# Column sums on GpSimd, spills issued by SyncE, softmax division on VectorE, in a perceiver block

## The chip, the cores and the metric

One Trainium2 chip, one core. The time is the device time of one execution in microseconds (us). Another execution was taken with the hardware profiler. It has its own time and a trace. Engines: TensorE (PE), VectorE (DVE), ScalarE (ACT), GpSimd (POOL) and SyncE (SP, which only issues DMAs).

## The reference, cut to what matters

For 16 batches (NB) of 64 latent rows (LQ) and 512 context rows (S), width 512 (D), everything float32:

```
ln  = layernorm(layernorm(x)) * g_l + b_l          # 1024 latent rows in all
xn  = layernorm(ctx) * g_x + b_x
q   = ln @ w_q ;  k, v = split(concat(xn, ln) @ w_kv)
x  += layernorm(softmax(q k^T / 8) v @ w_out) * g_o + b_o      # 8 heads of 64
x  += differential_attention(layernorm(x))
x  += fp4_ffn(layernorm(x))                        # weights quantised in blocks of 16
```

Two parts bear on the change. The layernorm of the context is folded into the weights: a context key is `rstd * (ctx @ Wf)`, with `Wf = g_x * w_kv - mean over rows of (g_x * w_kv)`. The folding needs the column sums of `g_x * w_kv`. The shift `b_x @ w_v` is carried as one more value row. In the same way, part of the latent norm's shift is taken out of the queries and comes back as the vector `b_x @ w_q` ("queries' shift").

## The kernel before, in words

Every engine runs one program written out by hand. The order of a program is the order of its work. Engines wait on counting semaphores only, so an instruction that waits holds up all that stands behind it on its engine. SP is such a program too: a DMA issue that waits holds up every later DMA of SP. Products that need accuracy are done as three passes of rounded halves (`mm3`, L142: hi*hi, hi*lo, lo*hi), with ACT rounding to `hi` and DVE subtracting to get `lo`.

**Stage A** (latents) ends about 92 us into the span. SP loads x in four tiles and one block of four, and then w_kv. ACT issues the four loads of w_q. DVE takes statistics and norms x, PE turns it (`turn_first_latents`, L471), and `first_queries` (L481) makes the first half of the queries. Between its chunks stand sixteen narrow float32 matmuls (L487) for the queries' shift. Then come keys and values of the latents, second half of everything, and `weight_means` (L522), an `mm3` of 12 matmuls per half of w_kv that gives the column sums in two PSUM rows. ACT copies these to `mean_row`. SP writes them to DRAM and reads them back spread over all partitions (`spill_means`, `spread_means`), and `fold_weight` on DVE (L917) uses them. Queries, latent keys and values go to DRAM scratch. POOL issues 20 of these spills (`spill_query` for both halves, `spill_latent_key` and `spill_latent_value` for the first) as soon as each is ready. SP issues the last eight, after `load_pack(0)`.

The SP program of stage A, in order: loads; context rows 0 (waits for the second half's turned latents); context columns 0; masks and constants; context rows 1; `spill_rstd(0)`, a write of 512 single floats; `spread_rstd(0)`, which waits for that write to land; `load_pack(0)`, which waits for all spills of queries and for those of the first half's keys and values; the last spills; context columns 1; w_out.

**Stage B** (cross attention) has 16 batches of 8 slots. Slots 0 to 3 project keys, slots 4 to 7 project values and make scores. One slot is 12 matmuls of 512 columns and small work. The softmax of head pair n of a batch goes through three slots. In slot n+4 PE makes scores, DVE takes the row maximum (`largest`, L938) and ACT the exponent. In slot n+5 DVE inverts the sum (`invert_sum`, L948) and ACT multiplies 128x576 by it (`normalise_p`, L1515), and in slot n+6 PE turns the result. Beside it, 34 tiles of ffn weights are quantised on DVE, 4 steps per slot. Each is turned on PE, split by ACT (`hi_of_weight`, L1555) and DVE (`lo_of_weight`, L1042), and POOL spills both halves with two DMAs (`spill_weight`, L1863). `hi_of_weight` waits for the spills of the tile before, since they share buffers. A tile is split at slot 4, 7 or 0 of an odd batch and at slot 2 or 5 of an even one.

In slot 3 of batch 0, DVE waits for all spills of stage A to land and then clears buffers that lie on their place (`zero_pack(1)`, L1240, called at L1310). Behind it on DVE stand the last keys and the first `largest`, which frees the PSUM bank for PE's second scores.

In each batch SP issues, in slot 4, the next context rows and `spill_rstd` (L1988), and in slot 5 `spread_rstd` (L1993), which waits for that write. `scale_k` of the next batch needs the result.

Stages C to E (differential attention, ffn) have no part in the change.

## Time and profile before

| | |
|---|---|
| time, median of 3 runs | 995.66 us (992.62 to 996.56) |
| the profiled execution's own time | 999.49 us |
| its span, first to last instruction | 997.7 us |
| PE busy | 954.4 us, 96% |
| DVE busy | 772.9 us, 77% |
| ACT busy | 440.2 us, 44% |
| POOL busy | 144.9 us, 15% |
| granted TensorE clock, mean | 0.995 |

PE's ends are modelled and overlap, so the share of busy time says less than the list of its waits. The clock is at 2.4 GHz except for two stretches, one of them in the middle of stage B.

### The profile page before, as it was taken

The numbers are of one execution on the slowest core, as the hardware profiler recorded it, in microseconds if no ns is written. First come the engines' busy times: TensorE is split into PE (matmuls) and PEld (weight loads), VectorE is DVE, ScalarE is ACT, GpSimd is POOL, SyncE is SP. The second block draws the span as 40 slices with busy tenths as digits, with TensorE's granted clock in tenths as the row PEclk, the third lists the DMA queues.
The fourth block names the chain that finished last, engine by engine and source line by source line (L and its number), as shares of the span: only waits on it lengthen the run. The fifth ranks groups of instructions, "written<-read, shape, count | busy, mean of one in ns | idle before, by whom it ended". The sixth has DMA issues, their size and how long they took to land.

```text
span 997.7 us, 16573 instructions
## 1 busy us (share of the span) xinstructions
PE 954.4 (96%) x6364; PEld 776.7 (78%) x6364; DVE 772.9 (77%) x1653; ACT 440.2 (44%) x848; POOL 144.9 (15%) x166
## 2 busy tenths in 40 slices
PE   5999899999999979999999999999999999999997
PEld 4778788787888868787888887777777678888885
DVE  6555677798788858887887884578888588999984
ACT  4533654664465445466446644633324322222221
POOL 1220011211111111111211211022322000000000
PEclk9999999999999999999999999999999999999999
DMA  5788576756667563685676557160001730000000
GB/s 213 197 251 186 160 143 151 164 111 181 162 111 183 136 164 99 155 169 118 169 155 148 120 141 184 39 222 23 1 1 59 289 118 11 11 11 11 11 11 21
DMA packets 91994, 120.04 MB, mean 120 GB/s; under 512 B 47366, under 2 KB 56198, under 8 KB 89612
## 3 DMA queue, kind: packets, MB, share of 16 engines
q1 hardware_dynamic: 83980, 93.30, 32.7%
q0 software_dynamic: 7360, 24.65, 13.2%
q8 instruction: 50, 0.82, 0.4%
q10 hardware_dynamic: 576, 1.05, 0.3%
q14 instruction: 28, 0.23, 0.1%
HBM read 89.04 MB, written 29.93 MB: 119 GB/s over the span
## 4 chain that ended last, share of the span: by engine, by line
PE 65%; DVE 15%; DMA 7%; issue 6%; ACT 5%; POOL 1%; SPq 0%; DVEq 0%; ACTq 0%
PE ps_banks L146 16%; PE ps_banks L148 15%; PE ps_banks L147 15%; PE ps_banks L462 5%; DMA scratch_rstd<-sb_rstd_b 4%; PE ps_banks L580 3%; PE ps_banks L661 3%; PE ps_banks L728 2%; PE ps_banks L729 2%; PE ps_banks L730 2%; DVE sb_kfull L894 1%; DVE sb_kT_lo L865 1%; DMA scratch_wdn<-sb_w_lo 1%; DVE sb_b_stats L826 1%; PE ps_banks L495 1%
## 5 line engine op out<-in xcount | busy, mean ns | idle before, releaser
L1430 ACT ACTIVATE sb_kT_hi<-sb_kfull 128x512 fp32r<-128x512 f32 x64 | 40.5, 632 | 164.5 <-DVE sb_kfull L894 164.5
L146 PE MATMUL ps_banks<-sb_zT_hi,sb_wkv_hi 128*128 128x512 f32 x256 | 106.9, 418 | 0.3 <-DVE sb_kfull L894 0.3
L148 PE MATMUL ps_banks<-sb_zT_hi,sb_wkv_lo 128*128 128x512 f32 x256 | 100.9, 394 | 0.0
L147 PE MATMUL ps_banks<-sb_zT_lo,sb_wkv_hi 128*128 128x512 f32 x256 | 100.4, 392 | 0.0
L147 PE MATMUL ps_banks<-sb_wkv_lo,sb_zT_hi 128*128 128x512 f32 x256 | 100.3, 392 | 0.0
L146 PE MATMUL ps_banks<-sb_wkv_hi,sb_zT_hi 128*128 128x512 f32 x256 | 100.1, 391 | 0.0
L148 PE MATMUL ps_banks<-sb_wkv_hi,sb_zT_lo 128*128 128x512 f32 x256 | 100.0, 390 | 0.0
L945 DVE CUSTOM_DVE_ANT_0 sb_probs<-ps_banks,sb_maskbias 128x576 f32<-128x576 f32 x64 | 48.1, 751 | 34.1 <-PE ps_banks L148 33.7
L146 PE MATMUL ps_banks<-sb_wgu,sb_z_hi 128*128 128x512 f32 (+1 forms) x192 | 73.7, 384 | 0.0
L147 PE MATMUL ps_banks<-sb_wgu,sb_z_hi 128*128 128x512 f32 (+1 forms) x192 | 72.1, 375 | 0.0
L148 PE MATMUL ps_banks<-sb_wgu,sb_z_lo 128*128 128x512 f32 (+1 forms) x192 | 72.0, 375 | 0.0
L894 DVE TENSOR_TENSOR sb_kfull<-ps_banks,sb_rstd_row 128x512 f32<-128x512 f32 x64 | 43.6, 681 | 26.6 <-PE ps_banks L148 17.2
L1517 ACT ACTIVATE sb_probs<-sb_probs,sb_row_inv 128x576 f32<-128x576 f32 x64 | 49.6, 775 | 27.7 <-DVE sb_row_inv L953 27.1
L148 PEld LDWEIGHTS ps_banks<-sb_zT_hi,sb_wkv_lo 128*128 128x128 f32 x256 | 48.4, 189 | 11.1
L146 PEld LDWEIGHTS ps_banks<-sb_zT_hi,sb_wkv_hi 128*128 128x128 f32 x256 | 48.5, 189 | 10.8 <-DVE sb_kfull L894 0.6
L865 DVE TENSOR_TENSOR sb_zT_lo<-sb_ctxT,sb_zT_hi 128x512 fp32r<-128x512 f32 x64 | 43.7, 687 | 16.2 <-ACT sb_zT_hi L1430 15.1
L148 PEld LDWEIGHTS ps_banks<-sb_wkv_hi,sb_zT_lo 128*128 128x128 f32 x256 | 48.1, 188 | 10.5
L1505 ACT ACTIVATE sb_v<-ps_banks,sb_rstd_b 128x512 f32<-128x512 f32 x64 | 43.6, 681 | 27.5 <-PE ps_banks L148 27.3
L147 PEld LDWEIGHTS ps_banks<-sb_zT_lo,sb_wkv_hi 128*128 128x128 f32 x256 | 48.7, 190 | 8.6
L146 PEld LDWEIGHTS ps_banks<-sb_wkv_hi,sb_zT_hi 128*128 128x128 f32 x256 | 48.0, 188 | 8.5
L147 PEld LDWEIGHTS ps_banks<-sb_wkv_lo,sb_zT_hi 128*128 128x128 f32 x256 | 48.0, 188 | 8.1
L1512 ACT ACTIVATE sb_probs<-sb_probs,sb_neg_max 128x576 f32<-128x576 f32 x64 | 49.4, 772 | 1.7 <-DVE sb_neg_max L945 1.4
(263 smaller groups left out, 2435.3 us busy)
## 6 DMA issues: line engine op xcount, KB each, us to landing
sb_ctx<-in_ctx SPq DMA_DIRECT2D x16, 1024.0 KB
sb_ctxT<-in_ctx_t SPq DMA_DIRECT2D x16, 1024.0 KB, 8.4
sb_wgu<-scratch_wgu SPq DMA_DIRECT2D x8, 1024.0 KB, 9.7
scratch_wgu<-sb_w_hi POOLq DMA_DIRECT2D x22, 256.0 KB
scratch_wgu<-sb_w_lo POOLq DMA_DIRECT2D x22, 256.0 KB
sb_wdn<-scratch_wdn SPq DMA_DIRECT2D x2, 2816.0 KB, 9.7
scratch_q<-sb_a_qk POOLq DMA_DIRECT2D x8, 512.0 KB, 7.2
sb_rstd_row<-scratch_rstd SPq DMA_DIRECT2D x16, 256.0 KB, 4.8
```

Of the source, the lines that this page charges most:

```text
L146: e.matmul(o, wh, xh, start=i == 0, stop=False)
L147: e.matmul(o, wh, xl, start=False, stop=False)
L148: m = e.matmul(o, wl, xh, start=False, stop=i == n - 1)
L462: m = e.transpose(psum[:, bank, k * P:(k + 1) * P], s, ident[:, :])
L580: m = e.matmul(o_space(r, n), value, p_t[j][:, k, r], start=k == CS, stop=k == CS - 1)
L865: e.tensor_tensor(lo, full, hi.bitcast(F32), ALU.subtract).then_inc(done)
L894: e.tensor_tensor(k_full[n % 2][:, :], psum[:, bank, :], rstd_row[:, :], ALU.mult).then_inc(drained[bank])
L945: e.tensor_tensor_reduce(blocks(probs[j][:, :], WIDE // 2), s_space[j], blocks(mask_bias[:, keys(b)], WIDE // 2), -1.0, F32_MAX, ALU.add, ...
L1430: e.activation(dst, src, ACT.Identity).then_inc(done)
L1505: e.activation(v_sb[b % 2][:, k, :], psum[:, bank, :], ACT.Identity, scale=rstd_b[:, b % 2, k:k + 1]).then_inc(drained[bank])
L1512: e.activation(probs[j][:, :], probs[j][:, :], ACT.Exp, bias=neg_max[:, n:n + 1], scale=-1.0, accum_out=row_sum[b % 2][:, n:n + 1]).then_i ...
L1517: e.activation(probs[n % 2][:, :], probs[n % 2][:, :], ACT.Copy, scale=row_inv[:, n:n + 1]).then_inc(p_normed)
```

## The change

- Column sums: POOL multiplies each of the four 128x512 chunks of w_kv by its column of g_x (and of b_x for the values) and adds them up (`weighted_sum`): three sums of 7 instructions. One float32 matmul of 128x128 ones against 128x512 then gives each sum on all partitions. `copy_means` becomes one ACT copy of 128x512 with scale 1/D, straight to `mean_all`. The DMAs of the means go. `b_x @ w_v` is a third such matmul at the end of stage A, and ACT copies it to its row of the value buffers.
- The queries' shift: all sixteen matmuls stand behind the first transposes, and DVE's reduction stands before it norms the second half.
- Tiles 0 and 2 of x and chunks 0 and 2 of w_q go by SP, tiles 1 and 3 and chunks 1 and 3 by ACT.
- All spills of POOL are issued by SP. The first half's queries and latent keys stand behind the load of context columns 0, the latent values behind the constants, the second half's queries behind `spread_rstd(0)`. A weight tile is spilled one slot after its split, behind what SP has in that slot.
- `normalise_p` moves from ACT to DVE: reciprocal and multiplication, now behind `largest` of the same slot.

```diff
             def turn_first_latents():
                 banks = [claim(("lnT", 0, c), ring_a) for c in range(C)]
+                shift_bank = claim(("qs",), ring_a)
...
+                for k in range(C):
+                    on.wait_ge(wq_landed[k], 16)
+                    for n in range(C):
+                        m = e.matmul(psum[:, shift_bank, n * C + k:n * C + k + 1], w_raw[:, k, n * P:(n + 1) * P], cols[:, 1, k:k + 1], start=True, stop=True)
+                m.then_inc(filled[shift_bank])
...
             def weight_means(part):
-                mm3(e, psum[0:2, bank, :], lambda c: (gb_hi[:, :, c], gb_lo[:, :, c]),
-                    lambda c: (wkv_hi[:, c, cs], wkv_lo[:, c, cs]), range(C)).then_inc(filled[bank])
+                on.wait_ge(g_summed, part + 1)
+                e.matmul(psum[:, bank, :], ones[:, :], sum_g[:, part * D:(part + 1) * D], start=True, stop=True).then_inc(filled[bank])
...
-            def invert_sum(b, n):
+            def normalise_p(b, n):          # on DVE
                 on.wait_ge(exped, idx + 1)
                 e.reciprocal(row_inv[:, n:n + 1], row_sum[i][:, n:n + 1]).then_inc(row_inverted)
+                on.wait_ge(row_inverted, idx + 1)
+                e.tensor_scalar(probs[j][:, :], probs[j][:, :], row_inv[:, n:n + 1], None, ALU.mult).then_inc(p_normed)
...
-                    if old and slot == 0:
-                        invert_sum(b - 1, 3)
-                    if cur and slot >= 5:
-                        invert_sum(b, slot - 5)
                     if cur and slot >= 4:
                         largest(b, slot - 4)
+                    if old and slot == 0:
+                        normalise_p(b - 1, 3)
+                    if cur and slot >= 5:
+                        normalise_p(b, slot - 5)
...
+            def weighted_sum(out, weights, gain, done):     # on POOL
+                for c in range(C):
+                    if c == 0:
+                        e.tensor_scalar(out, weights[:, 0, :], gain[:, 0:1], None, ALU.mult).then_inc(pool_chain.up())
+                        continue
+                    on.wait_ge(pool_chain.sem, pool_chain.value)
+                    e.tensor_scalar(term[:, :], weights[:, c, :], gain[:, c:c + 1], None, ALU.mult).then_inc(pool_chain.up())
+                    on.wait_ge(pool_chain.sem, pool_chain.value)
+                    e.tensor_tensor(out, out, term[:, :], ALU.add).then_inc(done if c == C - 1 else pool_chain.up())
...
             # SP, stage A
-            spill_means(0)
             load_rows(0)
-            spread_means(0)
             load_columns(0)
+            for n in range(C):
+                spill_query(0, n)
+            for n in range(C):
+                spill_latent_key(0, n)
             load_mask(0)
...
-            spill_means(1)
-            spread_means(1)
+            for k in range(4):
+                spill_latent_value(0, k)
             load_rows(1)
             spill_rstd(0)
             spread_rstd(0)
+            for n in range(C):
+                spill_query(1, n)
...
             # SP, stage B, in each slot
+                    if turned is not None:
+                        spill_weight(turned)
+                    turned = None
                     for job, step in WEIGHTS.get((b, slot), ()):
+                        if step == SPLIT_STEP:
+                            turned = job
                         if step == TURN_STEP and job + 2 < NJ:
                             load_weight(job + 2)
```

## Rows read from the trace of the kernel before

**Rows 1.** Waits of PE: us in total, times, longest us.
```profile
PE ps_banks L462 <- DVE sb_w_lo L865: 7.1, 1, 7.1
PE ps_banks L146 <- DVE sb_tile_lo L958: 4.6, 6, 1.1
```

**Rows 2.** Chain that ended last, the first 30 us: start us, us, what.
```profile
2.11 6.42 DMA sb_a_x<-in_x
...
10.48 3.02 PE ps_banks L477 x13
...
15.83 2.96 PE ps_banks L495 x12
18.80 0.79 PE ps_banks L487 x8
```

**Rows 3.** Timeline of PE: start us, us, instruction.
```profile
40.54 0.40 PE L146 MATMUL ps_banks<-sb_wkv_hi,sb_a_gb_hi 128*2 128x512 f32 x1
...
686.94 3.24 PE L661 MATMUL ps_banks<-sb_dwo,sb_tT 128*128 128x512 f32 x7 [0.41 <-ACT sb_tT L1623]
```

**Rows 4.** Timeline of SP, end of stage A and batch 0.
```profile
66.95 0.43 SPq L1990 DMA_DIRECT2D scratch_rstd<-sb_rstd_b  x1
83.21 0.32 SPq L131 DMA_DIRECT2D sb_rstd_row<-scratch_rstd  x1
...
88.85 3.93 SPq L131 DMA_DIRECT2D scratch_klat<-sb_a_qk  x4
...
109.80 0.33 SPq L131 DMA_DIRECT2D sb_ctx<-in_ctx  x1
111.30 0.38 SPq L1990 DMA_DIRECT2D scratch_rstd<-sb_rstd_b  x1
...
121.23 0.33 SPq L131 DMA_DIRECT2D sb_rstd_row<-scratch_rstd  x1
```

**Rows 5.** DMA issues: count, KB each, median us to landing.
```profile
scratch_klat<-sb_a_qk SPq DMA_DIRECT2D x4, 512.0 KB, 5.4
```

**Rows 6.** A stretch of stage A: us; busy PE, PEld, DVE, ACT, POOL; clock; DMA share; GB/s.
```profile
40.40:106.00 65.60, 65.60 (x302) 52.08 (x300) 36.30 (x70) 24.89 (x42) 7.84 (x11) 1.00 0.86 239
```

**Rows 7.** Timelines of DVE and PE in batch 0, at the clearing.
```profile
102.32 0.48 DVE L1242 MEMSET sb_qpack<- 64x512 uint32 x1
...
106.98 0.40 PE L146 MATMUL ps_banks<-sb_kT_hi,sb_qpack 128*128 128x288 f32 x1 [0.62 <-DVE sb_neg_max L945]
```

**Rows 8.** Batches 6, 7 and 8 of stage B, columns as in rows 6.
```profile
293.15:329.00 35.85, 35.20 (x241) 28.69 (x240) 29.80 (x72) 19.62 (x40) 6.19 (x8) 1.00 0.68 160
329.00:361.45 32.45, 32.45 (x235) 27.01 (x234) 28.58 (x68) 18.78 (x38) 5.25 (x6) 1.00 0.54 137
361.45:405.77 44.32, 37.03 (x241) 30.33 (x240) 30.08 (x73) 19.80 (x40) 6.76 (x9) 0.92 0.52 128
```

**Rows 9.** Timelines of POOL and ACT at the long stall.
```profile
363.08 0.71 POOL L131 DMA_DIRECT2D scratch_wgu<-sb_w_lo  x1 [11.00 <-issue]
...
370.52 0.60 ACT L1430 ACTIVATE sb_w_hi<-ps_banks 128x512 fp32r<-128x512 f32 x1 [10.30 <-DMA scratch_wgu<-sb_w_lo]
```

**Rows 10.** Waits on SP and ACT, whole span: us in total, times, longest.
```profile
SPq L131 <- DMA scratch_rstd<-sb_rstd_b: 159.7, 15, 15.8
ACT sb_w_hi L1430 <- DMA scratch_wgu<-sb_w_lo: 21.1, 5, 10.3
```

**Rows 11.** Groups by line: busy us, mean ns, idle us before them.
```profile
L839 DVE TENSOR_SCALAR sb_y_row<-sb_y_row,sb_lo_mv,sb_lo_rstd 128x512 f32<-128x512 f32 x7 | 3.8, 538 | 0.0
...
L1517 ACT ACTIVATE sb_probs<-sb_probs,sb_row_inv 128x576 f32<-128x576 f32 x63 | 48.8, 775 | 26.4 <-DVE sb_row_inv L953 25.8
...
L1876 POOL TENSOR_TENSOR sb_by_cos<-sb_by_cos,sb_by_sin 128x512 f32<-128x512 f32 x16 | 20.6, 1286 | 44.9 <-DVE sb_by_cos L1085 44.9
```

**Rows 12.** Timeline of DVE and PE in slot 6 of batch 7.
```profile
352.70 0.76 DVE L945 CUSTOM_DVE_ANT_0 sb_probs<-ps_banks,sb_maskbias 128x576 f32<-128x576 f32 x1 [0.58 <-PE ps_banks L148]
...
355.25 0.60 PE L462 MATMUL ps_banks<-sb_ident,sb_probs 128*128 128x128 f32 x4
```

More of the change, by code:

```diff
@@ L522, in weight_means, with value_shift @@
             def weight_means(part):
-                cs = slice(part * D, (part + 1) * D)
-                on.wait_ge(gb_lo_split, 1)
-                on.wait_ge(w_lo_split, part + 1)
+                on.wait_ge(g_summed, part + 1)
                 bank = claim(("gw", part), ring_a)
-                mm3(e, psum[0:2, bank, :], lambda c: (gb_hi[:, :, c], gb_lo[:, :, c]),
-                    lambda c: (wkv_hi[:, c, cs], wkv_lo[:, c, cs]), range(C)).then_inc(filled[bank])
+                e.matmul(psum[:, bank, :], ones[:, :], sum_g[:, part * D:(part + 1) * D], start=True, stop=True).then_inc(filled[bank])
+            def value_shift():
+                on.wait_ge(bv_summed, 1)
+                bank = claim(("vs",), ring_a)
+                e.matmul(psum[:, bank, :], ones[:, :], sum_bv[:, :], start=True, stop=True).then_inc(filled[bank])
             def project_k(b, n):
@@ L1736, in scalar_program @@
                 for slot in range(8):
+                    if b == 0 and slot == 4:
+                        place_shift_v(1)
                     if b == 0 and slot >= 4:
@@ L2038, in load_weight, with spill_query, spill_latent_key, spill_latent_value @@
                 copy_bits(e, w_in[job % 2][:, 0:width], src).then_inc(w_in_landed[job % 2], 16)
+            def spill_query(half, n):
+                i, b0 = staged(0, n), half * (NB // 2)
+                bank, nth = took["q", half, n]
+                on.wait_ge(drained[bank], nth)
+                copy_bits(e, q_spill[b0:b0 + NB // 2, :, n, :, :].rearrange("b p i k -> p b (i k)"),
+                          qk_stage[i][:, :, :, :].rearrange("p b i k -> p b (i k)")).then_inc(qk_spilled[i], 16)
+            def spill_latent_key(half, n):
+                i, b0 = staged(1, n), half * (NB // 2)
+                bank, nth = took["kl", half, n]
+                on.wait_ge(drained[bank], nth)
+                copy_bits(e, klat_spill[b0:b0 + NB // 2, :, n, :, :].rearrange("b p i k -> p b (i k)"),
+                          qk_stage[i][:, :, :, :].rearrange("p b i k -> p b (i k)")).then_inc(qk_spilled[i], 16)
+            def spill_latent_value(half, k):
+                t = 4 * half + k
+                bank, nth = took["vl", half, k]
+                on.wait_ge(drained[bank], nth)
+                copy_bits(e, vlat_spill[t * P:(t + 1) * P, :], v_stage[k][:, :]).then_inc(vl_spilled[half], 16)
+            def spill_weight(job):
+                kind, g, r, c0, width = JOBS[job]
+                k = width // P
+                bank, nth = took["w", job]
+                on.wait_ge(drained[bank], nth)
+                for part, src in enumerate((w_hi, w_lo)):
+                    dst = wgu_spill[g, part, :, :, r * P:(r + 1) * P] if kind == "gu" else \
+                        wdn_spill[part, :, c0 // P:c0 // P + k, r * P:(r + 1) * P]
+                    copy_bits(e, dst, src[:, 0:k, :]).then_inc(w_spilled, 16)
             def load_d_weight(n):
@@ L2045, in x_back @@
                 copy_bits(e, x3[:, t, :], a["x"][t * P:(t + 1) * P, :]).then_inc(x_again_landed[t % 2], 16)
-            for i in range(4):
+            for i in (0, 2):
                 copy_bits(e, x_in[:, i, :], rows("x")[:, i, :]).then_inc(x_landed[i], 16)
@@ L2050, in sync_program @@
             copy_bits(e, cols[:, :, :], a["cols"]).then_inc(consts_landed, 16)
+            for c in (0, 2):
+                copy_bits(e, w_raw[:, c, :], rows("w_q")[:, c, :]).then_inc(wq_landed[c], 16)
             copy_bits(e, x_in[:, 4:8, :], rows("x")[:, 4:8, :]).then_inc(x_landed[4], 16)
```

143 lines of the change are left out of this document (47 added, 96 removed).

## The prediction

> **What bounds the kernel now.** I read the list of waits first. PE is the engine that all others serve, and what little it waits for is spread thin: its longest wait after the start is one of 7.1 us for `w_lo`, and the largest repeated one is 4.6 us in six pieces for `tile_lo` [rows 1]. So an edit pays only where it takes matmuls off PE, opens PE earlier, or removes one of these waits. The windows by batch come next: an odd batch of stage B takes 32.45 us with PE never idle, an even one 35.85 us with 0.65 us idle, and batch 8 takes 44.32 us, 7.3 us idle, at a mean clock of 0.92 [rows 8]. The timelines around batch 8 name the cause: POOL issued the second spill of one weight tile 11.00 us late, waiting for nothing that the profile shows, and ACT stood 10.30 us in front of the next `w_hi`, which waits for that spill [rows 9]. The chain of the first 30 us is loads of x, transposes, queries [rows 2]. The last view is SP's own timeline, because the change hands twenty stage A spills and all weight spills to SP, whose waits stop everything behind them [rows 4].
>
> **Start and column sums, PE's own path.** The last tile of x lands 6.42 us after its issue [rows 2], behind three tiles and four chunks of w_q on two queues. With two tiles at the head of each queue it moves about one place of two up, some 2.5 us earlier, but two tiles' statistics and POOL's power stand between it and PE: I take 1.5 us (bounds 0 and 2.5). The transposes then end at 12.0 instead of 13.5. All sixteen shift matmuls now stand behind them: four groups of 0.79 us [rows 2], 3.2 us, so queries can start at 15.2 where they started at 15.83; ACT and DVE have the first chunk ready at 14.3 and are covered. Three groups between the chunks go (2.4 us). Queries end 3.0 us earlier, if DVE delivers chunks 2 and 3 and the split of w_k in time; POOL's sums beside it could take 1 to 2 us of that.
>
> `weight_means`: 12 matmuls at 2.96 us per 12 [rows 2], twice, become one float32 matmul each. The output projection's float32 matmuls of 512 columns show as two records each, 7 records in 3.24 us [rows 3], so 0.93 us per matmul. That is 2 x 2.0 us off, and one more, 0.93 us, for the value shift: 3.1 us off. PE's own path through stage A is 6.1 us shorter.
>
> The sums on POOL are 21 instructions of 128x512. Twelve are one-source, which no row shows; the nearest is the two-source sum of 1286 ns [rows 11]. At 0.7 to 1.6 us each that is 15 to 34 us; at 1.3 it runs from about 21 us to 48 us. Each is needed late: the first sum at 37 us when PE asks, the second at 51, the third where DVE folds the values. So POOL costs nothing here unless each takes over 1.6 us.
>
> By the Trainium skill (SBUF — State Buffer, "SBUF: two separate sides") VectorE and GpSimd share one port pair as an exclusive lock, also when VectorE has two SBUF inputs and GpSimd reads SBUF, and the later one blocks for the whole instruction. It speaks against this edit: each of DVE's splits under the sums could wait one POOL instruction, and PE would start the latent keys up to 2 us later. By that rule the part is worth 4 us, not 6.1; the sum below does not use either.
>
> **Spills on SP, stage A.** This eats that gain, I think. PE first asks for DVE in batch 0 at 106.98, where its second scores wait 0.62 us for the first row maximum, which stands behind the clearing at 102.32 [rows 7]. The clearing waits for every spill of stage A. Now follow SP. `weight_means(0)` began at 40.54 [rows 3]; with 12 matmuls and 16 transposes behind it the second half was turned at 45.0, now at 40.0. From there SP issues 9.1 MB in a row: context rows and columns 0 (2.1), queries (2.1), latent keys (2.1), constants and masks (0.7), values (1.05), rows 1 (1.05). Stage A moves 239 GB/s at a DMA share of 0.86 [rows 6], 278 GB/s when full: 33 us, to 75. Before, POOL had begun the queries and keys more than 10 us earlier, while no load ran. Behind rows 1 stands the rstd write. With the same rows load just ahead, issued at 109.80 and 111.30, it held `spread_rstd` until 121.23 [rows 4]: 11.4 us from the load's issue, of which a load of 1.05 MB takes 3.8 and first bytes 2. So 5 to 6 us behind the rows, at 80 to 81. Before, `spread_rstd` came at 83.21 with the queries' spills all issued. Now the second half's queries, 2.1 MB, go only then: 7.6 us and a landing, 90 to 91, and `load_pack(0)` waits for them. Before, pack and last keys were issued from 83.5, and the keys began at 88.85 [rows 4]. They begin now at 94 to 96, 5 to 7 us later, and the last spills (keys land 5.4 us after issue [rows 5]) with them. About 1 us of it is slack. I take the clearing 4.5 us later (bounds: 6.1 earlier, when SP keeps up, and 9 later). PE then stands at its second scores from about 100.3 to 111.5.
>
> By the Trainium skill (DMA: Bandwidth & Descriptors, "Queues, rings and completion order") descriptors of one ring are consumed in ring order, and only different queues take turns. By it, everything on SP's queue is a line, as I reckoned; if they shared instead, the rstd write would land by 67 and the clearing would not be late.
>
> An idle PE of 11 us may lose clock. In batch 8 the granted clock went to 1.2 GHz as PE stood 7 us: 0.92 over 44.32 us [rows 8] is 7.1 us at the lower level, 3.5 us of work. I take half, 1.7 us, since DVE limits batch 0 anyway (bounds 0 and 3.5).
>
> **Spills on SP, stage B.** The stall of batch 8 (7.3 us idle against 0.65 in batch 6, and 3.5 us by clock) came from POOL's issue [rows 9] and goes: 10.2 us. Of ACT's 21.1 us of such waits [rows 10], 10.8 are four others, at slot 7 of odd batches. There the tile split in slot 4 is ready just after SP begins to wait in `spread_rstd`, about 10.5 us per batch (159.7 in 15, [rows 10]); SP issues its spill only after that, and it lands some 4 us on. That is about where it lands today, when POOL issues at once but the DMA engines are busy: ACT waits a little longer, DVE's rstd row comes a little earlier. Together I take -2 us over stage B (bounds -5 and +14: no wait, and 2 us lost in each of seven odd batches). What waits behind the spill on SP are loads of weights and the next pack, each a slot or more early.
>
> **Division on DVE.** ACT loses 64 x 0.775 us [rows 11], but is not the bound. DVE gains 64 instructions of 576 elements with one scalar. A tensor_scalar of 512 with two takes 0.538 [rows 11]: 0.6 us, 2.4 us per batch. DVE is then busy 31.1 of 32.45 us in odd batches and 31.1 of 35.85 in even ones [rows 8], so it stays under PE in the mean. Within a slot: `largest` starts at 352.70 after waiting 0.58, PE turns the row before at 355.25 [rows 12]. Reciprocal (0.16) and multiplication behind 0.76 + 0.08 end at 354.3, 0.9 us early. It is late where DVE lags over 0.9 us, as in slot 5 of even batches with four quantising steps, and `tile_lo` [rows 1] is pushed by up to 0.6 us seven times. I take +3 us (bounds -1, the ACT waits that it frees, and +12, 0.75 us per batch).
>
> **Sum**, on the profiled execution's 999.5 us: +4.5 + 1.7 - 10.2 - 2 + 3 = -3.0, 996.5 us. The three timed runs lie 3 to 7 us under the profiled one, and a stall like batch 8's may be all or none of that. If they have it too, the median goes to 992.7; if they do not, it goes to 995.7 + 7.2 = 1002.9. POOL's issues hang in a way that the runs' scatter of 4 us fits, so mostly they do: I forecast 994 us, own range 988 to 1001.
>
> **Rivals.** A: SP keeps up. The spills drain faster than 278 GB/s or the rstd write lands sooner, DVE never waits at the clearing, and PE keeps its 6.1 us: 994 - 4.5 - 1.7 - 6.1 = 981.7, say 983. For it: the 278 GB/s is from a mix with POOL's queue. Against it: the rstd wait of 9.9 us in batch 0 had no POOL spill beside it. B, slower: SP is the bound of stage B. If the spill of slot 4 lands over 2 us later than today (the point is SP leaving `spread_rstd` 13 us after the write's issue, as it did at 83.21 after 16 us [rows 4]), ACT's `hi_of_weight` at slot 7 stands, then DVE's `lo_of_weight`, then the next keys: 2 us in each of seven odd batches, 14 us instead of -2, 1010. For it: the pattern of slots repeats. Against it: the slack of two slots in the other three places. C: DVE becomes the bound, +12 instead of +3: 1003.
>
> **Chances.** The forecast 0.40, A 0.30, B 0.17, C 0.13. A measurement of this kernel tells 0.5% (5 us) from no change, so faster is under 990.7, slower over 1000.6. Faster: A almost whole (0.28) and 0.09 of the forecast; slower: B 0.15, C 0.09, 0.03 of the forecast; same: the rest, 0.36. The range is 981 to 1006.
>
> **What would show it.** Right: queries start near 15.2 and end near 26.8; SP's timeline has `spread_rstd` at about 80 and the last keys at 94 or later; DVE idles 8 us or more before the clearing, PE waits at its second scores; no batch of stage B over 37 us; DVE's new instruction at 0.5 to 0.65 us. Wrong: the clearing before 100 (A); ACT idle over 4 us per odd batch before `w_hi` (B); PE waiting for `probs` from DVE in most slots (C); POOL's instructions over 1.6 us each, with PE waiting for its sums.

## The result, and the profile after

The kernel after takes 1020.02 us (median of four runs, 1014.12 to 1027.12), the kernel before beside it 995.6 us: ratio 1.0254, interval 1.0181 to 1.0327. The forecast was 994 us with a range of 981 to 1006, so the change is slower by 24 us where no change was forecast, and the time lies outside the range.

The profiled execution of after took 1022.4 us, its span is 1020.6 us. One event per batch, the start of its mask row on DVE, cuts both spans into pieces (us; the table is worked out from the timelines of DVE and PE):

| | before | after |
|---|---|---|
| transposes start on PE | 10.48 | 8.87 |
| first queries end | 29.66 | 32.4 |
| mask row of batch 0 | 95.14 | 100.39 |
| batch 0 | 26.90 | 33.16 |
| batches 1 to 14 together | 488.3 | 503.1 |
| mask row of batch 15 to the end | 387.4 | 383.9 |

5.3 us are lost ahead of batch 0, 6.3 in it, 14.8 in batches 1 to 14; 3.4 come back behind them. These are single profiles, and they scatter: with exactly after's code from batch 1 on, five profiles took 494.7 to 508.9 us for batches 1 to 14 (after, after_again, a_shift_back, a_pool_a, a_q1_first), and with exactly before's code four took 481.9 to 488.3 (before, b_loads, b_shift, b_spills_a). The means are 18.8 us apart.

**Start.** The chain that ended last in after (start us, us, what), against [rows 2]:

```profile
8.87 3.65 PE ps_banks L478 x16
12.52 6.62 PE ps_banks L484 x32
19.14 13.41 PE ps_banks L495 x48
```

Transposes begin 1.6 us earlier, as forecast. The block of shift matmuls (L484) takes 6.6 us instead of 3.2, so queries begin 3.3 us later than before and not 0.6 earlier. Until 23.8 us their matmuls start 0.43 us apart, from then on 0.23. The profile prints a granted clock of 1.00 for that stretch, but in the windows of after_again and b_shift below the same spacing stands beside 0.50, so I read it as the lower level (1.2 GHz) here too.

**Stage A on SP.** The timeline of SP in after, against [rows 4]:

```profile
46.93 9.48 SPq L131 DMA_DIRECT2D scratch_q<-sb_a_qk  x4
56.45 7.59 SPq L131 DMA_DIRECT2D scratch_klat<-sb_a_qk  x4
...
73.07 0.63 SPq L1975 DMA_DIRECT2D scratch_rstd<-sb_rstd_b  x1
87.53 0.32 SPq L131 DMA_DIRECT2D sb_rstd_row<-scratch_rstd  x1
87.89 5.54 SPq L131 DMA_DIRECT2D scratch_q<-sb_a_qk  x4
...
101.14 4.42 SPq L131 DMA_DIRECT2D scratch_klat<-sb_a_qk  x4
```

The first eight spills occupy SP for 17 us, 2.4 and 1.9 us each. Then SP stands 13.8 us for the rstd write, and the second queries go behind it. Last keys go at 101.14 instead of 88.85. SP's line itself starts at 46.07, when PE has turned the second half of the latents, and the forecast had that at 40.0. (POOL issued sixteen spills in stage A of before, eight of queries, four of keys and four of values, and SP eight more. The "20" and "twenty" of the description, the prediction and the expectations are a wrong count; the megabytes in the prediction are those of sixteen.) DVE and PE in batch 0, against [rows 7]:

```profile
96.27 0.48 DVE L1247 MEMSET sb_qpack<- 64x512 uint32 x1 [10.50 <-DMA scratch_q<-sb_a_qk]
...
113.67 0.48 DVE L1247 MEMSET sb_qpack<- 64x512 uint32 x1 [6.16 <-DMA scratch_vlat<-sb_a_v]
...
118.34 0.61 PE L146 MATMUL ps_banks<-sb_kT_hi,sb_qpack 128*128 128x288 f32 x1 [10.38 <-DVE sb_neg_max L950]
```

DVE waits twice, 10.5 us for the second queries' spills ahead of batch 0 and 6.2 us for the last values' in it; PE stands 10.4 us at its second scores. The first wait belongs to another clearing, `zero_pack(0)` ahead of batch 0 (`kernel.py` of before, L1291), which neither the description nor the prediction had. It moves the mask row; PE is held only by the second.

**Stage B.** Windows of batches 0, 6, 7 and 8 of after, columns as in [rows 6], against [rows 8]:

```profile
100.39:133.55 33.16, 21.62 (x111) 17.34 (x109) 20.04 (x51) 14.70 (x29) 1.38 (x1) 0.85 0.70 222
...
311.31:351.25 39.94, 37.42 (x244) 30.20 (x243) 31.92 (x76) 17.90 (x39) 2.20 (x2) 0.96 0.60 157
351.25:383.22 31.97, 31.97 (x232) 26.66 (x231) 30.54 (x73) 15.41 (x33) 3.25 (x3) 1.00 0.49 129
383.22:422.97 39.75, 37.42 (x243) 30.20 (x243) 31.93 (x76) 17.92 (x39) 2.20 (x2) 0.96 0.58 155
```

Batch 8 lost its stall (44.32 to 39.75) and odd batches are 0.5 us shorter, but the even ones grew from 35.85 to about 40, with 2.5 us of idle PE and a clock of 0.96. The waits of after (us in total, times, longest) name the chain, against [rows 1, 10]:

```profile
ACT sb_w_hi L1434 <- DMA scratch_wgu<-sb_w_lo: 27.5, 5, 6.6
DVE sb_w_lo L868 <- ACT sb_w_hi L1434: 21.8, 8, 4.4
PE ps_banks L462 <- DVE sb_w_lo L868: 17.1, 7, 3.7
ACT sb_w_hi L1434 <- DMA scratch_wdn<-sb_w_lo: 11.8, 2, 6.8
```

One instance, from the timelines of DVE, SP, ACT and PE around the start of batch 4 (237.30):

```profile
224.96 0.38 SPq L1975 DMA_DIRECT2D scratch_rstd<-sb_rstd_b  x1
226.70 0.69 DVE L868 TENSOR_TENSOR sb_w_lo<-ps_banks,sb_w_hi 128x512 fp32r<-128x512 f32 x1
...
234.71 0.33 SPq L131 DMA_DIRECT2D sb_rstd_row<-scratch_rstd  x1
235.08 0.52 SPq L131 DMA_DIRECT2D scratch_wgu<-sb_w_hi  x1
235.65 0.64 SPq L131 DMA_DIRECT2D scratch_wgu<-sb_w_lo  x1
...
242.55 0.60 ACT L1434 ACTIVATE sb_w_hi<-ps_banks 128x512 fp32r<-128x512 f32 x1 [6.61 <-DMA scratch_wgu<-sb_w_lo]
...
243.18 0.69 DVE L868 TENSOR_TENSOR sb_w_lo<-ps_banks,sb_w_hi 128x512 fp32r<-128x512 f32 x1 [3.76 <-ACT sb_w_hi L1434]
...
244.01 1.08 PE L462 MATMUL ps_banks<-sb_ident,sb_probs 128*128 128x128 f32 x4 [3.45 <-DVE sb_w_lo L868]
```

The tile is split at 227.4 and its spill issued from 235.08, once SP is out of `spread_rstd`; ACT's copy starts 6.9 us after the second half's issue, and PE waits 3.5 us. The same tile in the kernel before, from the timelines of POOL and ACT:

```profile
214.63 0.79 POOL L131 DMA_DIRECT2D scratch_wgu<-sb_w_lo  x1
...
225.93 0.60 ACT L1430 ACTIVATE sb_w_hi<-ps_banks 128x512 fp32r<-128x512 f32 x1 [2.40 <-DMA scratch_wgu<-sb_w_lo]
```

There the split ended at 213.6 and POOL issued right behind it. The landing took 11.3 us from the issue, longer than SP's 6.9, and still ACT's copy came 12.3 us behind the split and not 15.2, with 2.4 us of waiting and not 6.6. In after PE's wait is followed by a stretch at the lower clock level: the granted clock is 0.50 from 244 to 249 us. The means of 0.96 in batches 6 and 8 fit such a stretch in each.

The new instructions in the groups of after (busy us, mean ns, idle us before), against [rows 11]:

```profile
L958 DVE TENSOR_SCALAR sb_probs<-sb_probs,sb_row_inv 128x576 f32<-128x576 f32 x64 | 33.3, 520 | 2.3
...
L1896 POOL TENSOR_SCALAR sb_a_term<-sb_wkv_raw,sb_cols 128x512 f32<-128x512 f32 x9 | 17.9, 1988 | 0.9
```

### The profile page after: what moved, and what is told of

Its sections match the earlier page's. It is cut to its first block, busy times and chain, and to the rows that moved or that the text cites. A ratio compares the mean times of both kernels' runs of the same rounds, so it can differ in the third digit from the quotient of the medians.

```text
span 1020.6 us, 16509 instructions
## 1 busy us (share of the span) xinstructions
PE 966.3 (95%) x6346; PEld 786.6 (77%) x6346; DVE 808.2 (79%) x1716; ACT 401.8 (39%) x786; POOL 122.0 (12%) x102
## 4 chain that ended last, share of the span: by engine, by line
PE 55%; DVE 20%; DMA 14%; SPq 4%; issue 3%; ACT 2%; POOL 1%; DVEq 0%; ACTq 0%
PE ps_banks L146 13%; PE ps_banks L147 12%; PE ps_banks L148 12%; DMA scratch_rstd<-sb_rstd_b 8%; SPq L131 4%; PE ps_banks L462 4%; PE ps_banks L663 3%; DMA scratch_wgu<-sb_w_lo 2%; PE ps_banks L582 2%; PE ps_banks L730 2%; PE ps_banks L731 2%; PE ps_banks L732 2%; DVE sb_kT_lo L868 2%; DVE sb_probs L950 2%; DVE sb_kfull L897 1%
## 5 line engine op out<-in xcount | busy, mean ns | idle before, releaser
L146 PE MATMUL ps_banks<-sb_zT_hi,sb_wkv_hi 128*128 128x512 f32 x256 | 110.3, 431 | 0.0
L148 PE MATMUL ps_banks<-sb_zT_hi,sb_wkv_lo 128*128 128x512 f32 x256 | 103.7, 405 | 0.0
L147 PE MATMUL ps_banks<-sb_zT_lo,sb_wkv_hi 128*128 128x512 f32 x256 | 103.6, 405 | 0.0
L1887 POOL TENSOR_TENSOR sb_rstd_b<-sb_b_ve,sb_half_pow 128x4 f32<-128x4 f32 x16 | 18.3, 1146 | 341.8 <-DVE sb_b_ve L917 312.5
L462 PE MATMUL ps_banks<-sb_ident,sb_probs 128*128 128x128 f32 x256 | 41.0, 283 | 17.8 <-DVE sb_w_lo L868 17.1
L897 DVE TENSOR_TENSOR sb_kfull<-ps_banks,sb_rstd_row 128x512 f32<-128x512 f32 x64 | 43.5, 679 | 16.9 <-PE ps_banks L148 14.5
L148 PEld LDWEIGHTS ps_banks<-sb_wkv_hi,sb_zT_lo 128*128 128x128 f32 x256 | 48.5, 190 | 10.7
## 6 DMA issues: line engine op xcount, KB each, us to landing
sb_wdn<-scratch_wdn SPq DMA_DIRECT2D x2, 2816.0 KB, 10.5
```

The source lines that it names most:

```text
L146: e.matmul(o, wh, xh, start=i == 0, stop=False)
L147: e.matmul(o, wh, xl, start=False, stop=False)
L148: m = e.matmul(o, wl, xh, start=False, stop=i == n - 1)
L462: m = e.transpose(psum[:, bank, k * P:(k + 1) * P], s, ident[:, :])
L897: e.tensor_tensor(k_full[n % 2][:, :], psum[:, bank, :], rstd_row[:, :], ALU.mult).then_inc(drained[bank])
```

## The experiments

Fourteen other kernels and after once more, in four studies of one chip each; a ratio is always to the kernel before on the same chip, whose median moved between 995.2 and 999.6 us. The names: a_ starts from after, b_ from before, c_ from a mix. "us" made from a ratio use 995 us.

### 1. One part of after undone

**a_pool_w**: weight spills back on POOL.

```
-  (SP)   if turned is not None: spill_weight(turned)
+  (POOL) if step == SPLIT_STEP: spill_weight(job)
```

> The kernel after, with the spills of weight tiles issued by POOL again (two software DMAs per tile), all else as it is. Theory 1: the even batches of stage B grew (33 to 40-42.7 us) because SP issues a tile's spill only after its wait in spread_rstd, ACT's next w_hi waits for it, DVE's w_lo for that, PE for that. Then PE's 17.1 us of waits for w_lo fall to about 5, the even batches return to about 36 us each, and the time falls by 12 to 20 us to about 1002-1008 us, less where POOL's issue hangs again as in batch 8 of before. Theory 2: the division on DVE is what lengthens the even batches (DVE is busy 31.9 of 32 us there). Then they stay at 40 us and the time at 1018-1022 us.

Measured 1010.53 us, ratio 1.0107 (1.0069 to 1.0145): 1.5% off after. Batches 1 to 14 take 489.9 us together (503.1), PE's waits for `w_lo` are 7.1 us in two (17.1 in seven), and the stall of batch 8 is back (44.78 us). Theory 1 holds, theory 2 fails.

**a_spread7**: `spread_rstd` in slot 7.

```
-                    if b + 1 < NB and slot == 5:
+                    if b + 1 < NB and slot == 7:
                         spread_rstd(b + 1)
```

> The kernel after, with spread_rstd of the next batch moved on SP from slot 5 to slot 7, so that weight spills of slots 4 and 5 go out ahead of the wait. Theory 1 (SP's order): ACT's waits for the spills (27.5 + 11.8 us) mostly go, clock dips at half level in even batches go, time falls 10 to 20 us to 1000-1010 us; the rstd row lands later, but still before the next batch's keys need it; if it does not, DVE waits for rstd_row at the start of each batch and the gain turns into a loss of about 1-3 us per batch. Theory 2 (DVE's division): no change, 1018-1022 us. Theory 3 (spills are late because the DMA engines of one queue are full, not because SP waits): no change either, but ACT's waits stay at 27 us.

Measured 1007.78 us, ratio 1.0075 (1.0049 to 1.0101). Window of batch 6 and SP's timeline ahead of batch 4:

```profile
309.72:347.22 37.50, 35.95 (x243) 29.01 (x243) 31.54 (x77) 17.71 (x39) 2.20 (x2) 1.00 0.67 157
```

```profile
225.60 0.38 SPq L1975 DMA_DIRECT2D scratch_rstd<-sb_rstd_b  x1
...
228.05 0.52 SPq L131 DMA_DIRECT2D scratch_wgu<-sb_w_hi  x1
...
237.99 0.33 SPq L131 DMA_DIRECT2D sb_rstd_row<-scratch_rstd  x1
```

The spill goes ahead of the wait, ACT's waits for spills fall from 39.3 to 20.8 us and batch 6 is at the higher clock level throughout. PE's waits for `w_lo` fall from 17.1 to 0.6 us. Moving one line of SP's order took off 1.8%: theory 1 in the main, as half of ACT's waits stay. Since the queue is the same, theory 3 is out as the cause of the loss.

**a_shift_back**: shift matmuls and their reduction back in their old places.

```
                 for c in range(C):
+                    on.wait_ge(wq_landed[c], 16)
+                    for n in range(C):
+                        m = e.matmul(psum[:, shift_bank, ...], w_raw[...], cols[:, 1, c:c + 1], ...)
```

> The kernel after, with the sixteen one-column matmuls of the queries' shift back between the chunks of the first queries, and DVE's reduction of them back behind norm_latents and w_lo; all else as it is. Theory 1: as one block of 6.6 us behind the transposes they held PE at the lower clock level until 24.3 us. Back in place: queries start at 12.5-13.5 us instead of 19.0, at full clock from about 15-17 us, end 5 to 9 us earlier (24-28 instead of 32.4 us), and the time falls by 0 to 8 us, as far as SP's order in stage A does not give it back at the clearing. Theory 2: queries are late because DVE and ACT deliver the chunks late under POOL's sums. Then queries end at 30 us or later all the same.

Measured 1023.14 us, ratio 1.0223 (1.0179 to 1.0267): no gain that can be told. Queries started at 14.60, but at the lower level until 19.86, and ended at 31.17. Both theories fail in part: the lower level can come without the block (more below).

**b_norm**: before with the division on DVE.

```
+                e.reciprocal(row_inv[:, n:n + 1], row_sum[i][:, n:n + 1]).then_inc(row_inverted)
+                on.wait_ge(row_inverted, idx + 1)
+                e.tensor_scalar(probs[j][:, :], probs[j][:, :], row_inv[:, n:n + 1], None, ALU.mult)
```

> The kernel before, with the division of the probabilities done by DVE (reciprocal and multiplication right behind each other) instead of ACT; all else as it is. Theory 1: costs 0 to +4 us (995-1000 us); the multiplication itself takes 0.35-0.6 us, batches change by under 0.5 us. Theory 2 (the division makes DVE the bound of stage B): even batches grow by 3 to 5 us each, time +15 to +25 us, 1010-1020 us.

Measured 1000.63 us, ratio 1.0007 (0.9982 to 1.0032). Batch 6:

```profile
293.37:330.55 37.18, 35.88 (x243) 29.01 (x243) 31.64 (x77) 17.70 (x39) 6.29 (x8) 1.00 0.64 153
```

Batch 6 is 1.3 us longer than before, odd batches are 0.5 us shorter (31.99): the total is theory 1's, though batches move by more than its 0.5 us. The division alone isn't the cause.

### 2. One part alone, on the kernel before

**b_spills_w**: weight spills by SP (the first diff, turned round).

> The kernel before, with the spills of weight tiles issued by SP in the slot behind the split, as in the change; stage A's spills, the division and all else as before. Theory 1 (SP's order in stage B is the cause of the largest part of the loss): even batches grow from 35.8 to 40-42 us, batch 8 from 44.3 to about 40, time +8 to +18 us against before. Theory 2 (it needs the division on DVE as well, which takes DVE's slack): even batches grow by less than 2 us, batch 8's stall goes, time -5 to +3 us.

Measured 1005.93 us, ratio 1.0097 (1.0067 to 1.0128). Batch 6 takes 39.08 us with ACT's old division in place, and PE's waits for `w_lo` are 16.5 us in seven: the spills on SP suffice without the division, theory 1. This edit changes engine, queue and slot together; b_spills_w7 parts SP's wait from the rest.

**b_spills_a**: stage A's sixteen spills by SP.

```
             load_columns(0)
+            for n in range(C): spill_query(0, n)
+            for n in range(C): spill_latent_key(0, n)
...
+            for k in range(4): spill_latent_value(0, k)
             load_rows(1)
             spill_rstd(0)
             spread_rstd(0)
+            for n in range(C): spill_query(1, n)
```

> The kernel before, with stage A's twenty spills (queries, latent keys, latent values) issued by SP between its loads, as in the change; all else as before. Theory 1: SP's line in stage A (spills held at issue 1.9-2.4 us each, then the rstd write and its wait, then the second queries) puts the clearing and batch 0 off: first mask row at 98-101 instead of 95.1, batch 0 of 31-33 us instead of 26.9, time +7 to +13 us. Theory 2: what delays them in the kernel after is the slow start and POOL's sums (37.6 us), which come later than before: then this kernel's first mask row is at 95-97 and the time within 3 us of before.

Measured 1009.84 us, ratio 1.0142 (1.0114 to 1.017). SP's timeline and the window of batch 0:

```profile
81.44 0.66 SPq L1962 DMA_DIRECT2D scratch_rstd<-sb_rstd_b  x1
91.76 0.32 SPq L131 DMA_DIRECT2D sb_rstd_row<-scratch_rstd  x1
92.12 5.75 SPq L131 DMA_DIRECT2D scratch_q<-sb_a_qk  x4
```

```profile
104.47:140.26 35.79, 23.51 (x126) 19.20 (x126) 18.34 (x47) 15.73 (x31) 1.38 (x1) 0.86 0.66 207
```

The mask row of batch 0 is at 104.47 (95.14 before) and batch 0 takes 35.79 us (26.90): theory 1, and more than it asked. Here SP's line also has `spread_means`, for which SP stands 4.9 us (73.2 to 78.06).

**b_shift**: the shift matmuls as one block behind the transposes.

> The kernel before, with the sixteen one-column matmuls of the queries' shift as one block behind the first transposes, and DVE's reduction of them ahead of norm_latents; all else as before. Theory 1 (the block keeps PE at the lower clock level): the block takes 6-7 us instead of 3.2, queries start near 20 and run at the lower level until 24-25 us, end at 33-34 instead of 29.7, so stage A's end comes 3 to 4 us later, time 0 to +4 us. Theory 2 (the block is as fast as its four parts, 0.79 us each at the higher level): queries end at 29-30 us, time unchanged.

Measured 997.72 us, ratio 1.0023 (0.9999 to 1.0047). The timeline of PE:

```profile
13.82 4.02 PE L484 MATMUL ps_banks<-sb_cols,sb_a_w_raw 128*128 128x1 f32 x32
```

and the window behind the block:

```profile
17.70:23.70 6.00, 6.00 (x15) 4.74 (x16) 5.79 (x16) 4.82 (x7) 1.41 (x1) 0.50 0.00 0
```

Neither theory is right as put. The block took 4.0 us, and the level was low behind it: a granted clock of 0.50, which is 1.2 GHz, under fifteen matmuls in 6 us. Queries begin at 17.70 and end at 31.49 instead of 29.66. The time moves by 2.3 us (interval 0 to 4.7).

**b_loads**: x and w_q in turn on both queues.

```
-            for i in range(4):
+            for i in (0, 2):          (and i in (1, 3) on ACT's queue)
                 copy_bits(e, x_in[:, i, :], rows("x")[:, i, :]).then_inc(x_landed[i], 16)
```

> The kernel before, with the tiles of x and the chunks of w_q on both queues in turn; all else as before. Theory 1: transposes start 1.5 us earlier (8.9 instead of 10.5), but the clock reaches its higher level no earlier than before, so queries end at 28.5-30 us (29.66 before) and the time moves by less than 1.5 us either way. Theory 2: the 1.5 us come through, queries end near 28.1 and the time falls by 1.5 us. Either way the second query chunk's w_q must not be late; if it is, PE waits for it between chunks.

Measured 993.73 us, ratio 0.9977 (0.9959 to 0.9994). Transposes start at 8.74, queries end at 27.96 at the higher level, and the mask row of batch 0 comes at 93.44, 1.7 us earlier than before: theory 2.

### 3. Mending

**b_spills_w7**: before with weight spills on SP and `spread_rstd` in slot 7.

> The kernel before, with the weight spills issued by SP and spread_rstd in slot 7 instead of 5: the kernel with SP's weight spills alone took +10.7 us, and a_spread7 took about 16 us off the kernel after. Theory 1 (SP's wait for the rstd write is what delays the spills): even batches at 35.5-37.5 us, batch 8 without its stall (44.3 to 37), time -4 to -8 us against before, 987-991 us. Theory 2 (the hardware queue's spills are late for another cause, as SP's DMAs in line): even batches over 38 us and the time above before's.

Measured 998.15 us, ratio 0.9991 (0.9974 to 1.0009). Batch 8 takes 36.57 us, the other even batches of 4 to 12 take 36.1 to 38.4 (35.3 to 36.7 before). SP's wait was the loss of b_spills_w, but the stall of batch 8 is only traded for about 1 us in each of these even batches: between the two theories.

**a_pool_a**: after with only stage A's spills back on POOL, between the column sums.

```
+            for n in range(C): spill_query(0, n)          (behind the first sum)
+            for n in range(C): spill_latent_key(0, n)     (behind the second)
+            for k in range(4): spill_latent_value(0, k)   (behind the third)
+            for n in range(C): spill_query(1, n)          (behind the power of batch 0)
```

> The kernel after, with only stage A's twenty spills back on POOL, put between its column sums (queries' behind the first, keys' behind the second, values' behind the third). Theory 1 (SP's line in stage A costs 13-15 us): first mask row at 94-97 instead of 100.4, batch 0 of 26-28 us instead of 33, time -9 to -14 us against after, ratio to before 1.010-1.016. Theory 2 (the sums, 37.6 us on POOL, hold what follows): the spills are as late behind the sums, first mask row at 99 or later, and the ratio stays over 1.02.

Measured 1015.68 us, ratio 1.0163 (1.0136 to 1.019), 0.9% off after. The window of batch 0:

```profile
94.09:120.82 26.73, 25.30 (x139) 20.95 (x137) 20.28 (x51) 15.09 (x30) 1.41 (x1) 1.00 0.61 199
```

Batch 0 is whole again although the sums push the queries' spills from 29.75 to 34.56 us and the keys' from 35.58 to 49.43: theory 1. It ends 12.7 us earlier than in after, of which the time shows 9: batches 1 to 14 took 508.9 us in this profile, with the code that took 503.1 in after.

**c_sums**: a_pool_a with `spread_rstd` in slot 7 and the shift matmuls between the chunks.

> The kernel after with three parts mended: stage A's spills back on POOL between the sums, the shift matmuls back between the chunks, spread_rstd in slot 7. What is left of the change: column sums on POOL, loads on both queues, weight spills on SP, division on DVE. If the parts add up: queries end at 28-31 us by the clock's level, column sums 3 us less of PE, first mask row at 90-94, batch 0 of 26-27 us, even batches 37.3, no stall in batch 8: 985-990 us, ratio 0.990-0.996. If POOL's sums push its spills beyond what batch 0 allows, 995-1005 us.

Measured 992.56 us, ratio 0.9941 (0.9915 to 0.9967): 0.6% faster than the kernel before, and the best of the study. Window of batch 0:

```profile
90.17:122.72 32.55, 27.08 (x139) 22.36 (x137) 20.38 (x51) 15.10 (x30) 1.41 (x1) 0.95 0.66 209
```

Batch 0 starts 5.0 us earlier than before and is 5.7 us longer: it ends at 122.72, where before ended it at 122.04. The shorter path of PE is given back to the last keys' and values' spills, which SP issues at 88.3 and 92.6 as it did before: DVE waits 3.2 us for them at the clearing, where it did not wait before, and PE then 2.1 us at its second scores and 3.2 us for the first division (0.9 before). So the ratio is what was expected if the parts add up, but batch 0 is not.

**c_plain**: before with b_loads and b_spills_w7 together.

> The kernel before with two parts of the change and the later spread_rstd: loads on both queues and weight spills on SP, spread_rstd in slot 7. If the parts add up (-1.5 and -5 to -8 us): 986-989 us, ratio 0.991-0.993. Rival: batch 8 trades its stall for waits spread over the even batches (+0.5 to 1.5 us each), and the ratio is 0.996-1.000.

Measured 997.33 us, ratio 0.9969 (0.9948 to 0.9989), with batch 8 at 37.33 us and batches 4, 6, 10 and 12 0.7 to 2.9 us longer than before: the rival. Its profiled start was at the lower level until 19.90.

### 4. What was left open

**after_again**: after, on the chip of the next two.

> The kernel after, unchanged, beside the two others. All theories: ratio to before 1.018-1.033 as measured, queries at the lower clock level again until about 24 us, mask row 0 near 100 us, batch 0 near 33 us, even batches 40-42 us.

Measured 1018.95 us, ratio 1.0249 (1.0222 to 1.0276). Its block of shift matmuls and the window behind it:

```profile
12.24 4.04 PE L484 MATMUL ps_banks<-sb_cols,sb_a_w_raw 128*128 128x1 f32 x32
```

```profile
16.20:21.80 5.60, 5.60 (x14) 4.38 (x14) 5.43 (x13) 4.11 (x5) 2.15 (x2) 0.50 0.06 22
```

The same kernel needs 4.0 us for the block here and 6.8 in after by the same view (12.31 to 19.14). Queries end at 29.9 instead of 32.4, SP's line starts at 43.60 instead of 46.07, the last keys go at 98.55 and the mask row of batch 0 comes at 97.78, all 2.5 or 2.6 us earlier. Batch 0 takes 32.95 us as expected.

**a_q1_first**: the second queries' spills ahead of the wait.

```
             spill_rstd(0)
-            spread_rstd(0)
             for n in range(C):
                 spill_query(1, n)
+            spread_rstd(0)
```

> The kernel after, with the second half's four query spills issued by SP ahead of the wait in spread_rstd(0) instead of behind it. Theory 1 (that wait is what holds the clearing, as the prediction had it): DVE's wait of 10.5 us for these spills falls below 4 us, first mask row at 96-98 instead of 100.4 or batch 0 of 28-30 us instead of 33, time -3 to -7 us. Theory 2 (SP's line is late as a whole: held issues, the last keys and values behind it): spread_rstd only moves behind the spills, the clearing gains under 2 us and the time moves by less than 2 us.

Measured 1012.34 us, ratio 1.0188 (1.0157 to 1.0218). SP's timeline:

```profile
71.36 15.39 SPq L131 DMA_DIRECT2D scratch_q<-sb_a_qk  x4
86.80 1.36 SPq L131 DMA_DIRECT2D sb_rstd_row<-scratch_rstd  x1
```

DVE's wait fell from 10.4 to 7.6 us and the last keys went at 95.85 instead of 98.55; batch 0 ends 1.4 us earlier (129.32 against 130.73). So the wait is one part of it and the line as a whole the larger: theory 2 nearly. The time fell by 6 us, of which these 1.4 are explained by stage A; the profiled run has 7 us less in batches 1 to 14, where its code is that of after. That is inside the scatter of such profiles (494.7 to 508.9 us), so it is not shown that the edit brought it.

**c_rstd_pool**: c_sums' start, with the rstd write (slot 4) and its broadcast (slot 7) on POOL.

> The mended kernel (stage A's spills on POOL between the sums, shift matmuls between the chunks), with the rstd row's write and broadcast on POOL behind its own power (write in slot 4, broadcast in slot 7), so that SP waits for no rstd write at all; weight spills on SP. Theory 1 (SP's wait for the rstd write is all that makes SP's weight spills late): ACT's waits for spills fall from 19 us to under 8, even batches 36-37 us, time 2 to 6 us under c_sums, ratio 0.988-0.992. Theory 2 (the hardware queue's order and landings are what remains): even batches stay at 37.5-38.5 us, ratio 0.993-0.996. Theory 3: POOL's software issues hang as in batch 8 of before, now on the rstd row, which all the next keys need: DVE waits for the row by some us in many batches and the ratio is over 1.

Measured 1061.43 us, ratio 1.0672 (1.0633 to 1.071). Its waits:

```profile
PE ps_banks L146 <- DVE sb_kfull L897: 39.8, 14, 5.5
ACT sb_w_hi L1434 <- DMA scratch_wgu<-sb_w_lo: 14.9, 5, 3.4
```

Theory 3: the row came too late for the next keys, and PE waited for them. ACT's waits for spills, 14.9 + 5.9 us, are those of c_sums (12.8 + 6.4) though SP waits for no rstd write here. So in c_sums that wait is no longer what makes the spills late, and theory 1 fails. Why spills still land late was not settled.

## Why the prediction was wrong

**Where the forecast missed.** It had -3.0 us in the profile and the profile shows +22.9. Up to the end of batch 0 the forecast was +4.5 + 1.7 = +6.2, and batch 0 ends 11.5 us later (133.55 against 122.04): 5.3 us missed. Behind it the forecast was -10.2 - 2 + 3 = -9.2, and it is +14.8 - 3.4 = +11.4: 20.6 us missed. So the larger failure is stage B, the smaller the start of stage A.

**Start path: forecast -3.0, measured +2.7 in after and +0.3 in after_again.** The loads were right (-1.6 for -1.5). The failed step is "four groups of 0.79 us, 3.2 us, so queries can start at 15.2": the price was taken from groups that stood between full matmuls. From the start of the transposes to the end of the queries PE needs 19.2 us in before, b_norm and b_loads and 19.6 in c_sums. In the seven profiles with the block it is 20.8 to 23.9 (after 23.5), each with 4.8 to 6.2 us of queries at the lower level; the block itself took 6.8 us in four of them and 3.9 to 4.0 in three. Without the block six of ten profiles had some of the lower level as well (20.7 to 22.2), among them b_spills_w7, whose code up to there is that of before. So the block was never followed by a clean start, but how much of that it causes stays open: the ranges overlap, and the timed runs of b_shift show +2.3 us (0 to 4.7) and those of a_shift_back no gain.

**Column sums: forecast -3.1, measured -3.7.** From the end of the queries to the mask row of batch 0 it is 65.5 us in before, b_norm, b_loads, b_shift and b_spills_w, and 61.7 in a_pool_a and 61.8 in c_sums. POOL's one-source instruction took 1988 ns on average, over my bound of 1.6 us, and the sums 37.6 us (20.83 to 58.4). PE did not wait for them, since each is needed late.

**Stage A on SP: forecast +4.5 and +1.7, after PE's gain of 6.1 is used up, so 12.3 by itself; measured +14.1 alone (b_spills_a) and 9 when undone from after (a_pool_a).** The direction and the place were right, and the size within these two: clearing late, PE idle at its second scores from about 108 to 118.3. The line was right too, once it is counted from its start:

| | forecast | after | after_again |
|---|---|---|---|
| SP's line starts | 40.0 | 46.07 | 43.60 |
| `spread_rstd` issued | 80 to 81 | 87.53 | 84.56 |
| last keys issued | 94 to 96 | 101.14 | 98.55 |
| start to last keys | 54 to 56 | 55.1 | 55.0 |

The failed step is "the second half was turned at 45.0, now at 40.0". It rests on queries that end 3.0 us earlier; they ended 2.7 later, and the whole line moved with them. Bytes at 278 GB/s gave the right length although SP is held in the issue, 2.4 us per queries' spill where POOL took 0.9, and although the same 7.34 MB are 13056 packets on SP's queue (97036 in b_spills_a, 83980 in before) for 2048 on POOL's. Some luck is in it: 40.0 + 33 is 73 and not the 75 written, and of the 14.5 us from the rstd write's issue to `spread_rstd` no run tells how much is the line of bytes ahead and how much the write itself; before it was 16.3 us at this place (66.95 to 83.21). By the Trainium skill (DMA: Bandwidth & Descriptors, "Queues, rings and completion order"), descriptors of one ring are consumed in ring order; these traces fit that and don't prove it. The clock term was right: PE's matmuls start 0.43 us apart from 118.3 to 122.6, about 2 us lost for a forecast of 1.7.

**Spills on SP, stage B: forecast -10.2 - 2, measured +9.7 alone (b_spills_w).** The stall of batch 8 did go. The failed step is "it lands some 4 us on. That is about where it lands today". Issued 7.7 us behind the split, the spill of the instance above lands 6.9 us on, at 242.5: 15.2 us behind the split where it was 12.3 before. That is 2.9 us later, over the 2 us that rival B put as its point, and PE waits 3.5 us. Rival B had the mechanism, ACT's copy, then DVE's, then PE (though PE stands at the turning of the probabilities and not at keys); it was given 0.17. Its sign came, 39.3 us of ACT's waits in seven pieces. The reason that it named, `spread_rstd` leaving SP 13 us behind the write, was not met: 9.8 us here. It priced 2 us in each of seven; the waits of PE are 2.4 on average (17.1 in seven), and the lower level behind them comes on top: from before to after batch 6 grows by 4.1 us, 1.9 of it idle PE, and a_spread7 takes 2.4 off again. A second step of this term was wrong by its own rows: batch 8 stood only 8.5 us over batch 6 (44.32 against 35.85), so removing the stall could not give 10.2.

**Division: forecast +3, measured +0.7 (interval -1.8 to +3.2).** Its multiplication takes 0.520 us for a guess of 0.6. DVE is busier in even batches, 31.6 us in b_norm where it was 29.8; the 31.1 that the prediction gave for them should have been 32.2 by its own numbers. Whether the spills on SP cost more because of it is not shown: in batches 1 to 14 they add 10.7 us without the division (b_spills_w's 495.0 against a mean of 484.3 in four profiles) and 12.6 with it (a mean of 503.1 in five against 490.5 in b_norm and a_pool_w), and the five alone are 14.2 us apart.

**Do the parts add up?** From the ratios: loads -2.3, shift block +2.3, stage A's spills +14.1, weight spills +9.7, division +0.7, column sums -3.7 by the profiles: 20.8 us, against 25.3 by the ratio of after. Each ratio has an interval of 2 to 3 us either way and that of after 7, so they agree, and nothing more can be read from the rest. The 3.4 us gained behind the mask row of batch 15 are not explained: that piece is 385.7 to 387.4 us in the seven profiles with the old division and 383.8 to 385.5 in those with the new (c_rstd_pool apart), but b_norm, the division alone, has 385.5.

**Chances.** Faster 0.37 for a forecast that already held two terms against the change was too much: every part that paid (loads, sums) was worth 2 to 4 us, while the two moves to SP were open upwards by 12.5 and 14. And rival B had 0.17 and a price of 1010 us, while the range ended at 1006.

## What to carry to other kernels

Before a transfer is moved to another queue, list what that queue's engine waits for around it: behind a wait of 10 us for a small write, the spill of a buffer that three engines hand on was issued 7.7 us late, and moving the wait by two slots took off 1.8%, the largest gain of any single edit. Bytes priced a line of large transfers well (55 us in stage A), but not one transfer for whose landing others wait: for that take its issue and its landing on that very queue. A line's start is a forecast of its own, and an error in it moves everything behind. An earlier start in a stage whose end is set by the last spills gives back little beyond that point: c_sums starts batch 0 5.0 us earlier and ends it 0.7 us later, while the 1.7 us of b_loads were still 1.4 at the end of batch 0.

## What the runs showed of the hardware

- **POOL and DVE take turns.** Timelines of both in after:

```profile
25.10 1.35 POOL L1898 TENSOR_TENSOR sb_a_sum_g<-sb_a_sum_g,sb_a_term 128x512 f32<-128x512 f32 x1
26.55 3.48 POOL L1896 TENSOR_SCALAR sb_a_term<-sb_wkv_raw,sb_cols 128x512 f32<-128x512 f32 x1
...
31.51 1.57 POOL L1896 TENSOR_SCALAR sb_a_term<-sb_wkv_raw,sb_cols 128x512 f32<-128x512 f32 x1
```

```profile
25.22 3.38 DVE L868 TENSOR_TENSOR sb_wkv_lo<-sb_wkv_raw,sb_wkv_hi 128x2048 fp32r<-128x2048 f32 x1
```

  DVE's split, 2.28 us in before, begins behind POOL's sum and ends at 28.60, 2.2 us after that sum's end at 26.45; POOL's next, 1.57 us at 31.51, ends at 30.03, 1.4 us behind DVE's. By the Trainium skill (SBUF — State Buffer, "SBUF: two separate sides"), whoever comes second waits for the whole instruction: the trace agrees, at 1.1 us for DVE here. It didn't cost PE anything.
- **Clock level at the start.** Identical code starts its queries at the higher level in one execution and at the lower in another (before at 15.83, b_spills_w at 16.14 until 18.85), and the block of one-column matmuls took 6.8 us in after and 4.0 in after_again.
- **Packets.** The queues of before, then those of b_spills_w (packets, MB, share of 16 engines):

```profile
q1 hardware_dynamic: 83980, 93.30, 32.7%
q0 software_dynamic: 7360, 24.65, 13.2%
```

```profile
q1 hardware_dynamic: 118860, 110.60, 38.6%
q0 software_dynamic: 2048, 7.34, 2.7%
```

  The same 17.3 MB of weight spills are 5312 packets on POOL's queue and 34880 on SP's, 6.6 times as many. Whether that is why SP is held at issue and the landings stay long was not tried alone.
